# A post-norm attention and mixture-of-experts block: wider mask products, four row slots, and tails behind the maxima

## What is computed

```python
q = (x @ Wq.T + bq).reshape(B, T, H, D)          # B=2, T=1024, H=16, D=8; k and v alike
scores = jnp.einsum('bqhd,bkhd->bhqk', q, k) * attn_scale[0]
scores = jnp.where(mask[None, None], -jnp.inf, scores)   # hides from a query all earlier 64-token chunks and the later tokens of its own
attn = jax.nn.softmax(scores, axis=-1)
out = jnp.einsum('bhqk,bkhd->bqhd', attn, v).reshape(B, T, C)
x = _layernorm(x + out @ Wo.T + bo)

scores = jax.nn.sigmoid(xf @ gate_weight.T)       # 32 experts in 8 groups; 4 groups, then 6 experts are kept
combine = ...                                     # their weights, scaled to a sum of 2.5
for gu, dn, c in experts:                         # I = 64
    acc = acc + c[:, None] * ((silu(xf @ gu[:I].T) * (xf @ gu[I:].T)) @ dn.T)
x = _layernorm(x + acc + shared_expert(x))
```

## Time and profile before

| | us |
|---|---|
| median of three runs | 492.0 |
| lowest, highest | 490.45, 492.75 |
| profiled execution | 491.96 |
| its span | 490.0 |
| PE busy in the span | 422.9 (86%) |
| DVE busy | 343.7 (70%) |
| ACT busy | 220.7 (45%) |
| POOL busy | 131.6 (27%) |

### The profile page before, as it was taken

How to read it: one execution, slowest core, us unless ns; L and a number is a source line. 1 busy time by engine, 2 the same in 40 slices (tenths; PEclk the granted TensorE clock), 3 DMA queues, 4 the chain that set the end, 5 groups by cost and what they waited for, 6 DMA issues and landing times.

```text
span 490.0 us, 7996 instructions
## 1 busy us (share of the span) xinstructions
PE 422.9 (86%) x2856; PEld 218.9 (45%) x2856; DVE 343.7 (70%) x763; ACT 220.7 (45%) x299; POOL 131.6 (27%) x232
## 2 busy tenths in 40 slices
PE   6339979998698789798899997789999999999992
PEld 2225432433233233232333452467767666666661
DVE  3826978997588758589586448167768967865763
ACT  4600026675467647467477678322235233223220
POOL 4000014826545557444335434000000000000000
PEclk9855558999689979799799999899999999999998
DMA  4352430020211202101000000143213233443330
GB/s 142 131 183 96 113 96 3 4 93 7 62 51 34 84 7 71 50 3 61 7 1 3 1 1 3 44 137 88 106 70 107 102 119 105 135 134 101 110 108 21
DMA packets 27180, 34.26 MB, mean 70 GB/s; under 512 B 5893, under 2 KB 16261, under 8 KB 27141
## 3 DMA queue, kind: packets, MB, share of 16 engines
q1 hardware_dynamic: 26512, 33.41, 21.7%
q10 hardware_dynamic: 628, 0.34, 0.3%
HBM read 29.08 MB, written 4.46 MB: 68 GB/s over the span
## 4 chain that ended last, share of the span: by engine, by line
PE 60%; DMA 10%; DVE 9%; SPq 9%; POOL 4%; issue 4%; ACT 2%; POOLq 0%; DVEq 0%; ACTq 0%
PE ps L1235 12%; PE ps L1140 10%; PE ps L1100 8%; SPq L516 7%; PE ps L1207 6%; PE ps L1209 6%; PE ps L1208 6%; DVE mx L827 6%; DMA rows_k<-scratch 5%; PE ps L1123 4%; DMA w_raw<-in_unitT 2%; PE ps L1104 2%; PE ps L1160 2%; SPq L550 1%; ACT probs L727 1%
## 5 line engine op out<-in xcount | busy, mean ns | idle before, releaser
L827 DVE TENSOR_REDUCE mx<-ps 128x1 f32<-128x512 f32 (+3 forms) x320 | 180.9, 630 | 56.3 <-PE ps L1104 53.7
L727 ACT ACTIVATE probs<-ps 128x1024 f32<-128x1024 f32 (+2 forms) x160 | 143.5, 943 | 82.9 <-PE ps L1123 82.2
L1100 PE MATMUL ps<-rows_k,rows_q 48*128 48x512 bf16 (+3 forms) x384 | 111.9, 378 | 35.2 <-DMA rows_k<-scratch 26.7
L1140 PE MATMUL ps<-probs,Vg 128*32 128x512 f32 (+3 forms) x768 | 87.0, 526 | 7.5 <-POOL probs L625 6.5
L795 ACT ACTIVATE sg<-ps 128x512 f32<-128x512 f32 x68 | 40.8, 599 | 101.5 <-PE ps L1209 100.3
L1123 PE MATMUL ps<-rows_q,rows_k 51*128 51x512 bf16 (+3 forms) x384 | 72.9, 350 | 3.8 <-issue 2.5
L1207 PE MATMUL ps<-x1hi,w_hi 128*128 128x512 f32 x136 | 74.9, 551 | 0.0
L1100 PEld LDWEIGHTS ps<-rows_k,rows_q 48*128 48x128 bf16 x384 | 31.7, 99 | 95.5 <-DVE mx L827 55.3
L1035 DVE TENSOR_TENSOR au<-ps,sg 128x512 f32<-128x512 f32 x64 | 44.1, 689 | 38.0 <-PE ps L1235 37.0
L1235 PE MATMUL ps<-hh,w_down 128*128 128x512 f32 x136 | 69.8, 595 | 0.8 <-DVE hh L1040 0.8
L621 POOL TENSOR_SCALAR_AFFINE_SELECT probs<-probs 64x512 f32<-64x512 f32 x64 | 42.6, 666 | 69.0 <-ACT probs L727 66.6
(11 more groups left out here) (106 smaller groups left out, 316.7 us busy)
## 6 DMA issues: line engine op xcount, KB each, us to landing
comb_rows<-weights SPq DMA_DIRECT2D x128, 128.0 KB, 2.9
scratch<-oT SPq DMA_DIRECT2D x8, 384.0 KB, 3.0
w_raw<-in_unitT SPq DMA_DIRECT2D x17, 128.0 KB, 2.3
rows_q<-scratch SPq DMA_DIRECT2D x16, 96.0 KB
rows_k<-scratch SPq DMA_DIRECT2D x16, 96.0 KB
w_down<-in_unitT SPq DMA_DIRECT2D x1, 1088.0 KB, 7.7
xT<-in_xT SPq DMA_DIRECT2D x4, 256.0 KB, 3.9
rows_q<-scratch SPq DMA_DIRECT2D x16, 64.0 KB
```

The lines of the kernel that those rows point to most:

```text
L727: act.activation(dst, src, ACT.Exp).then_inc(exps_ready, 1)
L827: dve.tensor_reduce(m_[:, part, j:j + per, qt], src, AX.X, ALU.max).then_inc(max_read, 1)
L1100: mm = pe.matmul(bank(b, m, at), rows_q[f:f + ROWS, s, p + qt * P:p + (qt + 1) * P], rows_k[f:f + ROWS, s, p + k0:p + k0 + m], start=True, ...
L1140: mm = pe.matmul(ps[STRIP * j:STRIP * (j + 1), VALUES * BANK:VALUES * BANK + m], Vg[:, g % 2, kt, j, :], probs[:, (NB * g + b) % SLOTS, j, ...
```

## The change

- **Mask.** One product for each head with 128 rows of contraction and 128 columns (`identb` by `mask_qk`) takes the place of the two with 64 rows and 64 columns. The first part of a query tile is now at most 256 columns for two heads in one bank, the rest goes in parts of up to 512; there are still 40 units a group. The number of score products of the maxima goes from 384 to 512, that of the mask products from 512 to 256. DVE keeps three partial maxima and joins them by one reduction (`join`).
- **Slots and order.** NS = 4, and the planner has no `LEAD`: maxima go first whenever they can. Its estimates are new.
- **Start.** All eight projections go to eight banks, the value projections follow at once, ahead of the first maxima. ACT's queue loads the biases, the two mask tables and the `rows_k` half of group 0 (`load_k`); SP loads its `rows_q` half (`load_q`). The last two of the eight parts are split by POOL (`split_rest`) instead of DVE. `w_raw` has four buffers, and seven of the expert weights are split before the first tops.
- **Constants.** The loads of `x`, `wo`, `bo`, the gate and `w_down` stand behind the first `store_max` and the rows of group 3.
- **Last group.** Its maxima run in two halves of the queries, each with a top of its own; SP and ACT store six small rows each (`store_half`).
- **Tails.** They stand behind all maxima in chunks of 512 tokens, each with a router pass of its own. Chunk 0 is routed before the experts; chunk 1 goes as far as its logits; the rest of chunk 1 and chunks 2 and 3 are spread in the expert loop. The loop's first two silus stand ahead of the last output copy on ACT.

The core of the diff:

```diff
-NS = 3
+NS = 4
+RAW = 4
-        for part, (k0, m) in enumerate([(P * qt, min(n, BANK)), (P * qt + BANK, n - BANK)]):
+        for part, most in ((0, BANK // PAIRS), (1, BANK), (2, BANK)):
+            m = min(n, most)
...
+SPLIT_FROM = NG - 1
+LOW, HIGH = range(KT // QH - 1, -1, -1), range(KT - 1, KT // QH - 1, -1)
+MAXU = [max_units([*LOW, *HIGH] if g_ >= SPLIT_FROM else [*HIGH, *LOW]) for g_ in range(NG)]
...
+QUAD = 4
+CHUNK_STEPS = ([("out", t) for t in range(QUAD)] + [("turn", 0), ("proj", 0), ("stat", 0), ("aggr", 0), ("norm", 0),
+                                                   ("x1T", 0), ("logit", 0)]
+               + [("route", t) for t in range(8)] + [("comb", 0)])
...
+    steps.append(("top", len(TOPS) - 1, 0))
+    return steps + tail + [(kind, 1, i) for kind, i in CHUNK_STEPS[:ROUTED]]
...
+LOOP_FIRST = {1: ROUTED, 2: 0, 3: 0}
+LOOP_BASE = {1: 0, 2: 3, 3: 18}
...
-        if k / len(MSEQ) * NG - i["e"] / NE > LEAD and i["e"] < len(ev):
-            return far
...
+            for n in range(NC):
+                sp.wait_ge(parts_ready, n + 1)
+                store_parts(n)
+
+            load_rows(0)
+            load_rows(1)
...
+            for u in range(RAW):
+                load_unit(u)
+            load_rows(2)
...
+                    store_max(g)
                     if g == 0:
-                        sp.dma_start(w_down[:, :, :], a["unitT"][:, :, 2 * P:]).then_inc(down_loaded, 16)
+                        load_rows(3)
+                        load_consts()
...
+            copy_projection(5)
+            act.wait_ge(ones_set, NS)
+            act.wait_ge(k_stored[0], 32)
+            load_k(act, 0)
...
                     if part == 0:
-                        for c in range(2):
-                            mm = pe.matmul(bank(b, CHUNK, at + c * CHUNK), pick[f:f + CHUNK, c, :],
-                                           mask_k[f:f + CHUNK, :], start=False, stop=c == 1)
+                        mm = pe.matmul(dst[:, at * m:at * m + P], identb[:, :], mask_qk[:, :], start=False, stop=True)
...
-            for k in range(COMB, len(TAIL)):
-                tail_step(0, k)
-            pe.wait_ge(output_copied, QH * NG)
```

More of the change, by code:

```diff
@@ L41, with max_units @@
 ONES = float.fromhex("0x1.007f000000000p+0")
-def max_units():
+def max_units(qts):
     units = []
-    for qt in range(KT - 1, -1, -1):
-        n = T - P * qt
-        for part, (k0, m) in enumerate([(P * qt, min(n, BANK)), (P * qt + BANK, n - BANK)]):
[L51 to L54, removed]
+    for qt in qts:
+        k0, n = P * qt, T - P * qt
+        for part, most in ((0, BANK // PAIRS), (1, BANK), (2, BANK)):
+            m = min(n, most)
+            if m:
+                units += [(js, qt, k0, m, part) for js in ([(0, 1), (2, 3)] if 2 * m <= BANK else [(0,), (2,), (1,), (3,)])]
+            k0, n = k0 + m, n - m
     return units
@@ new lines, with max_steps @@
+ON_BANK = ("unit", "top", "out", "turn", "proj", "x1T", "logit", "comb")
+ROUTED = CHUNK_STEPS.index(("route", 0))
+def max_steps():
+    steps = []
+    tail = [(kind, 0, i) for kind, i in CHUNK_STEPS]
+    for g in range(NG):
+        for n in range(NM):
+            steps.append(("unit", g, n))
+            if n == TOP_AFTER and g:
+                steps.append(("top", len(TOPS_BEFORE[g]) - 1, 0))
+            if g >= SPLIT_FROM and n == NLOW + TOP_AFTER:
+                steps.append(("top", len(TOPS_BEFORE[g]), 0))
+            if tail and (g, n) >= TAIL_FROM and n % 2:
+                steps.append(tail.pop(0))
+    steps.append(("top", len(TOPS) - 1, 0))
+    return steps + tail + [(kind, 1, i) for kind, i in CHUNK_STEPS[:ROUTED]]
@@ L137, in attention_order @@
     fills = list(FILLS)
-    tt = [(0, n) for n in range(COMB)]
-    i = {"e": 0, "m": 0, "v": 0, "t": 0}
-    lag = {"out": 800, "turn": 900, "proj": 1100, "x1T": 1500, "logit": 700, "comb": 0}
-    streams = {"e": ev, "m": MSEQ, "v": vv, "t": tt}
+    for _ in range(FIRST_FILLS):
+        pool_order.append((fills[0][0], 0, fills.pop(0)[1]))
+        clock["pool"] += 1300
+    pool_order.append(("values", 0, 0))
+    clock["pool"] += 800
+    i = {"e": 0, "m": 0, "v": 0}
+    streams = {"e": ev, "m": MSEQ, "v": vv}
@@ L167, in run_sides @@
             elif what == "top":
-                top_read[g] = end + hop
-                todo["pool"].append(("split", g, 0, end + hop, 1500))
+                read["top", g, 0] = end + hop
+                todo["pool"].append(("split", g, 0, end + hop, 2500))
             elif what == "split":
                 split_done[g] = end + hop
+                if TOPS[g][1] is not None:
+                    todo["act"].append(("rows", g, 0, end + hop, 2000))
+            elif what == "root":
+                root_done[g] = end + hop
+            elif what in CHUNK_KINDS:
+                act_done[what, g] = end + hop
             elif what == "mask":
@@ L388, in build @@
         max_rows_loaded = [sem(f"max_rows_loaded_{n}") for n in range(NS)]
+        late_rows_loaded = [sem(f"late_rows_loaded_{n}") for n in range(NS)]
+        max_set = sem("max_set")
         max_scores = sem("max_scores")
@@ L665, in bias_x @@
                 pool.wait_ge(x_biased, q + 1)
-            values(0)
+            for n in (6, 7):
+                split_rest(n)
             for what, g, n in pool_order:
@@ L1259, in _ @@
                     down(i - 2)
[L1260 to L1261 removed]
+                for at, step in LOOP:
+                    if at == i and step[0] in ON_BANK:
+                        loop_step(step)
             back(NC - 1)
```

853 lines of the change are left out of this document (472 added, 381 removed).

## The result

The changed kernel takes 525.1 us (median of 4 runs, 516.2 to 541.9) against 491.2 us of the kernel before in the same session, 1.069 times as long. By its two fast runs alone, 516.2 and 521.4, it is 1.058 times as long, with a 95% interval of 1.051 to 1.065. The forecast was 482, the range 457 to 498. The four runs of the changed kernel lie 26 us apart, and the longer a run is, the lower is its mean clock: 0.904 at 516.2 us, 0.895 at 521.4, 0.877 at 528.9 and 0.845 at 541.9.

A forecast was written before the change was run, and what follows sets the result against it. PE was taken as the bound once the row stall goes, DVE next. 69.4 us to first exponentials, 7 x 29.5 for groups, 30.9 last group, 4.2 gap, 167.4 and 2 behind, plus 1.96 gave 482.4 us; range 457 to 498.

The forecast's parts named there:

- the start: Before the first exponentials: first maxima at 28.5 us, then 61 units of 0.67 us, so first exponentials at 69.4 us.
- the half clock: Rival: PE falls to half clock in stretches of maxima or around mask products; 507 us, chance 0.10; nothing in the sum.
- the base of a group: PE's need in a group without the stall and without the new mask's cost: 23.7 us, forecast 29.5 in all.
- the last tops: Last group: halving its tops gains nothing; ACT's stores, up to 3.8 us for each half, only in the range.
- The price of a change of rows: Around each mask product in the attention, PE switching between few rows and 128 costs 0.10 us, 48.8 us in all.
- The first rival: At the mask products the change of rows costs nothing, DVE bounds groups at 25.0 us; 452 us, chance 0.16.
- The second issuer: At the start, ACT's queue issues row transfers beside SP, taking 3.7 us off the first maxima's 32.6.
- 61 units: Units ahead of the first exponential product in PE's order, formerly 55, taken at 0.67 us each, bounds 0.59 and 0.71.
- Slots: In the groups, four row slots remove the 3.6 us stall and the half clock behind it, 5.7 us a group.
- Constants on SP: Loads moved behind the first tops' stores cost nothing before group 1, due at 98.9 us; 5 us in the range.
- The gap ahead of the experts: From the last values to the second product down: 4.2 us instead of 12.6, as chunk 0 is routed earlier.

The follow-up runs named there:

- spread kernel: The changed kernel with, in every group except the last, the 16 units with a wide mask standing evenly between the 24 without: 502.6 us.
- small masks: The changed kernel with each head's mask added by two products with 64 rows, as in the kernel before, instead of one with 128: 471.9 us.
- whole top: The changed kernel with two 64-row mask products a head, and the last group's top taken whole and stored by SP alone: 463.4 us.
- one mask for two heads: The changed kernel with one wide mask product opening the bank for both heads of a unit: 483.3 us; with the last top undivided 472.8 us.

## Why the prediction was wrong, step by step

Here is the sum of the prediction, beside the profiled runs of the spread kernel, which has all wide masks and 7 us at half clock behind its first exponentials, and of the changed kernel (spans, us):

| | forecast | spread (501.7 us) | changed (541.9 us) |
|---|---|---|---|
| to the first exponentials | 69.4 | 73.0 | 79.1 |
| six groups | 177.0 | 186.0 | 215.9 |
| seventh group | 29.5 | 34.5 | 38.4 |
| last group | 30.9 | 32.5 | 32.5 |
| behind the last values | 173.6 | 174.0 | 174.0 |

The forecast is 42.7 us under the median. Some 16 of these are the falls of the clock, as above. The other 26 or so are in the sum itself: 9.7 in the start, 9.0 in the price of six groups, 5.0 in the seventh, 2.0 behind it. So without the falls the kernel would still have taken some 509 us, slower than before and outside the range. Two things failed: the half clock, which the sum put at nothing, and terms of the sum that were too small, above all the start, the base of a group and ACT's issues for the last tops.

- **The price of a change of rows** held: 0.105 us, where the earlier trace rows gave 0.09 to 0.10. The first rival, that the change is free here, is refuted: small masks save 5 us a group at full clock (31.0 to 26.0). The Trainium skill states that a change of the tiling mode drains the engine (TensorEngine Tiling (Array Packing), Tiling Modes, Key Properties). The 0.105 us agree with that, but don't show a drain, as the weight loads above fill the same time.
- **The base of a group** was too low. I took PE's need as 23.7 us, by a stretch without a stall, and it is some 25: 125.08 busy in five groups with small masks. With 6.0 for the mask that makes 31, which the spread kernel shows. I had 31 as a bound and chose 29.5. It is 1.5 us a group, 9.0 in six. The small-mask kernel has the 128 further score products too, 16 a group, which I put at nothing; whether they or the stretch of 20 us made the base too low, no run tells.
- **The half clock** is the step that failed most: the sum had nothing for it. I gave the rival 0.10 and 507 us on the argument that the clock stayed at 1.0 between 279 and 310. In that stretch there are no maxima, so it says nothing about runs of masked scores. Rows that do were at hand: maxima alone stayed at half clock for 36 us with PE 89% busy. The falls cost some 16 us of the median, where the rival reckoned with 25, and the time swings by 26 from run to run; the rival's 507 was too low because its other terms were the sum's. My reading that the clock falls behind a stall was too narrow: it also fell with PE 97 to 98% busy.
- **The start** failed in two terms. The second issuer was to bring the first maxima to 28.5; they came at 33.6. The Trainium skill states that SP's and ACT's transfers run on the same 16 engines, and that a second issuer saves issue time alone (Trainium Kernel Development and Optimization, Key Constraints); I had told it as a bound of 0.4 us. In the runs here even the issue time wasn't won: first maxima at 34.8 with two issuers, at 30.8 with SP alone. And 61 units took 0.75 us each, where I took 0.67 and bounded them at 0.71. A change cost no more at half clock than I said: with the same products ahead of the first exponentials, PE is busy 42.07 us with wide masks and 31.61 with small ones and the whole top, 0.09 for each of 112 changes. The bounds took PE or DVE as full, and neither was: in 45.5 us PE is busy 42.07 and DVE 34.28, and PE waits 3.3 us for DVE. I said that what stands ahead in PE's order sets the first exponentials; that held for the wide mask, while behind small masks POOL's splits did.
- **Slots**: right in kind (no wait of the maxima for rows) and near in size: 5.7 us a group, 40 in seven, against 45.7 with three slots and small masks.
- **The last tops**: wrong by a term that I had named. ACT's issues were "up to 3.8 us" for each half in the range and nothing in the sum; a whole top gains 8.5 us with small masks and 10.5 with one mask for two heads, in the seventh group and not in the last. In the spread kernel the seventh group is 5.0 us over the forecast.
- **Constants on SP** at no cost held: in the changed kernel no wait of PE for the second tops' stores stands among its waits behind 95 us, the longest of which is 2.8 us, for exponentials. **The gap ahead of the experts** held: the second product down starts at 369.68, 3.7 us behind the last values, where 4.2 were forecast, and from the last values to the end it is 174.0 for 173.6.

What the change's parts are worth, by pairs of kernels that differ in one of them:

| part | kernels | us |
|---|---|---|
| fourth slot | three slots, small masks, against four | -45.7 |
| wide mask, its changes of rows | spread wide masks against small masks | +30.7 |
| wide mask in runs: some 16 by the clock, 6 by the order at the start | changed kernel against spread wide masks | +22.5 |
| last top by halves with ACT's issues | small masks, halves against whole | +8.5 |
| first keys issued by ACT; the ranges of the runs overlap | whole top, ACT against SP | +3.2 |
| seven weight units ahead of the first top | seven against three | +3.6 |

The pairs stand on different neighbours, so the column is no sum.

What stays open: why keys issued by ACT land later even without group 1's rows in the way, why a fall comes at one group's masked scores in one run and at another's in the next, and whether a change of rows costs its 0.105 us by emptying the engine or by a weight load that can't run beside the product ahead.

## What to carry to other kernels

Two small products that keep the contraction rows of their neighbours can be cheaper than one wide product that changes them: count the changes in PE's order, not the products. Short products between such changes shouldn't stand in a run; spread them, and read the clock line before calling a full PE healthy. Before a second engine issues transfers, see what its own queue holds up: here each issue took ACT 0.6 to 0.8 us, in the chain that PE waited for.

## What the runs showed of the hardware that I had not expected

- The granted clock fell to 1.2 GHz (0.5) with PE 97 to 98% busy, within 4 us of the start of a run of short products with a change of rows between any two, and stayed there for 30.7, 34.1 and 20.5 us. In the kernel before with wide masks it stayed for 98.8 us with PE at 100%, behind a wait of 2.25 us.
- The same products, spread among others, kept 2.4 GHz for 155 us.
- The time at half clock differs from run to run of one program, 99 to 167 us by the mean clocks, and moves its time by 26 us in 525.
